# A product over 8 rows widened to 128 rows with zeros, and two transfers of a slotted tensor sent in the other order

## The chip, the cores and the metric

The kernel runs on one core of a Trainium2 chip. The metric is the device time of one execution in microseconds (us), the median of several runs. Engines are named as in the profile: PE (TensorE, matmuls), PEld (its weight loads), DVE (VectorE), ACT (ScalarE), POOL (GpSimd) and SP (SyncE, which here issues nearly all DMAs, and shows as SPq).

## What is computed

The input x is 8 batches of 512 tokens by 128 features, float32. Two layers follow each other:

```
xn = layernorm(x)
x  = x + [xa + concat(linear_attention(h), window_attention(h)) @ Wout] + ternary_ffn(xn)      # layer 0; h = rmsnorm(xa), xa = xn
xn = layernorm(x)
x  = x + causal_attention(LN(xn) ...) @ Wo + bo + sum_e gates[t,e] * (gelu(xn @ W1[e] + b1[e]) @ W2[e] + b2[e])   # layer 1
```

`gates` has, for each token, the softmax of the two largest of eight router logits and zero for the other six experts. The part `gates @ b2`, an (512 x 8) by (8 x 128) product for each batch, is computed apart from the experts' matrices, together with the causal attention's output projection `attn @ Wo`.

## The kernel before

Everything is written engine by engine, with semaphores set by hand. Work runs batch by batch, in a software pipeline. One pass of the loop over the batches (`Fori(1, LAST)`, six passes, b = 1 to 6) does four stages in this order on every engine:

- `linear_stage`: scores of the linear attention of batch b, and, interleaved, the row maxima (`causal_max`) of the causal attention of batch b-1.
- `causal_stage`: scores and weighing of the causal attention of batch b-1, and the window attention's row maxima of batch b.
- `slide_stage`: window attention's scores of batch b (32 units), and between them the end of batch b-1's causal attention (unit 18: `mix_causal`, which adds `gates @ b2` and `attn @ Wo` in one PSUM bank; DVE's `add_mixed` adds it to `y`, and SP's `store` writes y out), and projections of batch b+1.
- `dense_stage`: the dense feed-forward layers of batch b+1 and the projections k2 and q2 for the causal attention of batch b.

Around the loop stand an opening, a first pass without a batch before it, a last pass, and a tail with the causal attention of batch 7 alone. `mix_causal` so runs eight times: six in the loop, once in the last pass, once in the tail. After the tail come 78 expert tiles (`expert_tiles`, `load_tiles`, `add_tile`), which start once the last y is stored.

`mix_causal` (lines 624 to 633) issues, for each of four token tiles t of 128, first the product of `gatesT` and `b2` (line 631, 8 rows) and then that of `attnT` and `wo1` (line 632, 128 rows), both into the same 128 x 128 part of the bank. Every float32 matmul is two MATMUL records with two LDWEIGHTS in the profile, so the unit is 16 records. `weigh` (line 609) follows three units later with the fourth and third pair of heads' probabilities, for which it waits on POOL's `mask_slide` (lines 1097 and 1099) and DVE's `mask_middle` (line 1333).

Heads are laid out in slots of 32 rows by way of DRAM. For q2 and k2, ACT's `split_hi` writes the high part of the projection from PSUM to SBUF (k2 first, then q2), DVE's `split_lo` the rest, and SP then does the following. `split_and_send` waits for the high part, issues two DMAs of it, waits for the low part and issues a third (lines 395 to 402, 256 KB each). `fetch` reads the slots back: k2 in four DMAs (line 406, 192 KB each), q2 in one of 1024 KB (line 408). In the end of SP's `body` the order is: send k2, send q2, fetch k2 (after all three sends of k2 have landed), fetch q2 (after those of q2), wait for that fetch to land, fetch q1 of the next batch. PE waits for both k2 and q2 (`slots_k2`, `slots_q2`) ahead of the first `causal_max`: in `linear_stage` after a lead of 12 linear units, the third layer among them, and in `tail_stage` with nothing but `prefix` ahead.

At the start POOL clears buffers (lines 1205 to 1210) and raises `cleared`; ACT issues 21 loads of later weights (line 1049). DVE waits for `cleared` ahead of line 1599.

Of the kernel before, what the change touches and what calls it, by code (L numbers as in the profile page):

```python
# [15 lines left out]
P = 128  # L16
NB, T = 8, 512
# [5 lines left out]
FC = 4  # L23
E = 8
# [18 lines left out]
SETUP_LOADS, FIRST_LOADS, LATER_LOADS, EXPERT_LOADS = 5, 10, 21, 2  # L43
# [165 lines left out]
def build(nc, dram, out):  # L209
    with ExitStack() as ctx:  # L210
        def sb(name, shape, dt=F32, where=ctx):
            return where.enter_context(nc.sbuf_tensor(name, shape, dt))
# [10 lines left out]
        bv1, bo1 = (sb(n + "_s", [P, P]) for n in ("bv1", "bo1"))  # L223
        wq1, wk1, wv1, wo1 = (sb(n + "_s", [P, P]) for n in ("wq1", "wk1", "wv1", "wo1"))
        wgT = sb("wgT_s", [P, E])
        b1, b2 = sb("b1_s", [P, E * FC]), sb("b2_s", [E, P])
        ident = sb("ident_s", [P, P])
        causal_neg, slide_neg = sb("causal_neg_s", [P, T], BF16), sb("slide_neg_s", [P, WQ], BF16)
        slide_top = sb("slide_top", [P, WIN])
        earlier = sb("earlier_s", [P, E * E])  # L230
# [17 lines left out]
        lg, lgs, ex, exs, gates, rank = (sb(n, [P, NT, E]) for n in ("lg", "lgs", "ex", "exs", "gates", "rank"))  # L248
        above, equal = (hrow[:, n:n + 2, :].rearrange("p a (b e) -> p (a b) e", e=E * E) for n in (0, 2))
        m1, gsum, rsum = (sb(n, [P, NT]) for n in ("m1", "gsum", "rsum"))  # L250
        gatesT = sb("gatesT_s", [E, T])

        picks, place = sb("picks", [P, NT + 1, K2 * E]), sb("place", [P, NT, K2 * E])
        base, base0 = sb("base", [P, K2 * E]), sb("base0", [P, K2 * E])
# [64 lines left out]
        S = {name: ctx.enter_context(nc.semaphore(name)) for name in counts}  # L319


        def due(name, sequence, count):
            (b, ahead), each = sequence, counts[name]
            return b * each + (ahead * each + count)
# [11 lines left out]
        def full_sem(run, unit):  # L336
            return S[f"full{PLACE[run[0]][unit][0]}"]

        def taken_sem(run, unit):
            return S[f"taken{PLACE[run[0]][unit][0]}"]  # L340

        def full_at(run, unit):
            return in_bank(run, unit) + 1

        def taken_at(run, unit):
            return in_bank(run, unit) + 1

        def bank_of(run, unit):
            return bank[PLACE[run[0]][unit][0]]
# [23 lines left out]
        def _(sp):  # L373
# [22 lines left out]
            def send(name, part, slots):  # L396
                view = scratch[name].rearrange("h (s d) t -> s h d t", d=D)
                for s in slots:
                    sp.dma_start(view[s], part.bitcast(F32)).then_inc(S[f"sent_{name}"], 16)
# [10 lines left out]
            def split_and_send(run, sequence, name):  # L410
                halves = parts_of[name]
                sp.wait_ge(S[f"hi_{name}"], due(f"hi_{name}", sequence, 1))
                send(name, halves[0], (0, 2) if name in ("k1", "k2") else (0, 1))
                sp.wait_ge(taken_sem(run, name), taken_at(run, name))
                send(name, halves[1], (1,) if name in ("k1", "k2") else (2,))

            def fetch_sent(sequence, name):
                sp.wait_ge(S[f"sent_{name}"], due(f"sent_{name}", sequence, SENT))
                fetch(name)

            def place_max(run, unit, mrow, to, sem):
                sp.wait_ge(taken_sem(run, unit), taken_at(run, unit))
                for i in range(HG):
                    row = ROWS * i + 3 * D
                    sp.dma_start(to[row:row + 1, :, :].rearrange("p g (n t) -> p (g n) t", t=P).bitcast(F32),  # L425
                                 mrow[G * NT * i:G * NT * (i + 1), :].bitcast(F32)).then_inc(S[sem], 16)

            def store(run, result_of):
                sp.wait_ge(taken_sem(run, "mixed_causal"), taken_at(run, "mixed_causal"))
                sp.sem_inc(S["unread"], 1)  # L430
                sp.dma_start(out_v[result_of], y[:, :, :]).then_inc(S["stored"], 16)

            def load_x(after_norm_of, which):
                sp.wait_ge(S["xa_ready"], due("xa_ready", after_norm_of, 1))
                sp.sem_inc(S["unread"], 1)
                sp.wait_ge(S["xn1"], due("xn1", after_norm_of, 1))
                sp.sem_inc(S["unread"], 1)
                sp.wait_ge(S["hrow1"], due("hrow1", after_norm_of, 1))
                sp.sem_inc(S["unread"], 1)
                sp.dma_start(x_in[:, :, :], x_v[which]).then_inc(S["x_loaded"], 16)  # L440

            def body(run, before, this, after):
                part, b = run
                if before and this:
                    place_max(run, "causal_max", mrow_c, Q2, "placed_c")
                if this:
                    place_max(run, "slide_max", mrow_s, Q1, "placed_s")
                if after:
                    for name in ("q1", "k1", "qm1"):
                        split_and_send(run, (b, 1), name)  # L450
                if this and after:
                    load_x((b, 1), (b + 2) & (NB - 1))
                if before and this:
                    store(run, b - 1)
                if after:
                    if this:
                        sp.wait_ge(taken_sem(run, SLIDE_UNITS[-1]), taken_at(run, SLIDE_UNITS[-1]))
                    fetch_sent((b, 1), "k1")
                    fetch_sent((b, 1), "qm1")
                if this:  # L460
                    split_and_send(run, (b, 0), "k2")
                    split_and_send(run, (b, 0), "q2")
                    if before:
                        sp.wait_ge(S["heads_out1"], due("heads_out1", (b, -1), G))
                        sp.sem_inc(S["unread"], 1)
                    fetch_sent((b, 0), "k2")
                    if after:

                        sp.wait_ge(S["sent_q1"], due("sent_q1", (b, 1), SENT))
                        sp.sem_inc(S["unread"], 1)  # L470
                    fetch_sent((b, 0), "q2")
                if after:

                    if this:
                        sp.wait_ge(S["slots_q2"], due("slots_q2", (b, 0), 16))
                        sp.sem_inc(S["unread"], 1)
                    fetch_sent((b, 1), "q1")
# [23 lines left out]
            set_keys("k1", "keys1_cleared", 2)  # L501
            load_x((0, 0), 1)
            body(("opening", -1), *PARTS["opening"])
            set_keys("k2", "keys2_cleared", 1)
            body(("first", FIRST), *PARTS["first"])
            with sp.Fori(1, LAST) as b:
                body(("steady", b), *PARTS["steady"])
# [405 lines left out]
        def _(act):  # L913
# [120 lines left out]
            def weigh_tile(i):  # L1034
                act.wait_ge(S["tile_out_full"], i + 1)
                if i >= OB:
# [3 lines left out]
            later_loads = [(sh1[:, :], dram["sh1"]), (h1T[:, :, :], dram["h1T"].rearrange("(c p) n -> p c n", p=P)),  # L1040
                           (sh2[:, :], dram["sh2"]), (h2T[:, :, :], dram["h2T"].rearrange("(c p) n -> p c n", p=P)),
                           (s3, dram["s3"].partition_broadcast(P)), (w3T[:, :, :], dram["w3T"].rearrange("(c p) n -> p c n", p=P)),
                           (wout[:, :, :], dram["wout"].rearrange("a p n -> p a n")), (gamma[:, :], dram["gamma"]), (beta[:, :], dram["beta"]),
                           (wq1[:, :], dram["wq1"]), (wk1[:, :], dram["wk1"]), (wv1[:, :], dram["wv1"]), (bq1[:, :], dram["bq1"]), (bk1[:, :], dram["bk1"]),
                           (bv1[:, :], dram["bv1"].partition_broadcast(P)), (wgT[:, :], dram["wgT"]), (b1[:, :], dram["b1"]),
                           (bo1[:, :], dram["bo1"].partition_broadcast(P)), (earlier[:, :], dram["earlier"]), (b2[:, :], dram["b2"]),
                           (wo1[:, :], dram["wo1"])]
            for dst, src in later_loads:
                act.dma_start(dst, src).then_inc(S["later_weights"], 16)  # L1049
            assert len(later_loads) == LATER_LOADS  # L1050
            act.wait_ge(S["setup_done"], 1)
            act.wait_ge(S["first_weights"], 16 * FIRST_LOADS)
            slide_stage(("opening", -1), False, False, True)
# [22 lines left out]
        def _(pool):  # L1076
# [130 lines left out]
            pool.memset(V2[:, :, :, D:D + 1], 1.0)  # L1207
            pool.memset(euler[:, :, :], math.e)
            pool.memset(causal_neg[:, 0:T - P], 0.0)
            pool.memset(half_neg[:, :], -0.5).then_inc(S["cleared"], 1)  # L1210
            pool.wait_ge(S["setup_done"], 1)
            power((0, 0), 1)
# [19 lines left out]
        def _(dve):  # L1232
# [27 lines left out]
            def take(run, unit, to, view=lambda x: x[:, :]):  # L1260
                dve.wait_ge(full_sem(run, unit), full_at(run, unit))
                dve.tensor_copy(to, view(bank_of(run, unit))).then_inc(taken_sem(run, unit), 1)
# [190 lines left out]
                                         in1=hidden_a[c], op0=ALU.mult, op1=ALU.mult).then_inc(taken_sem(run, f"up{c}"), 1)  # L1453

            def take_gates(run):
                take(run, "gatesT", gatesT[:, :], lambda x: x[0:E, :])

            def linear_stage(run, before):
                _, b = run
# [217 lines left out]
```

## Time and profile before

| | us |
|---|---|
| Median of 3 runs | 1498.56 |
| Lowest, highest | 1495.23, 1499.37 |
| Profiled execution | 1501.17 |
| Span of its trace | 1499.3 |
| PE busy | 1330.5 (89%) |
| DVE, ACT, POOL busy | 817.6, 707.5, 603.3 |
| Mean granted TensorE clock | 0.934 |

The span is the time from the first to the last instruction of the profiled execution; 1.9 us lie around it. Start times in the rows below are us from the start of the span. A busy time is that of an engine's instructions; matmuls overlap, so the starts of neighbouring matmuls tell more than the durations.

### The profile page before, as it was taken

To read this page: it belongs to the slowest core of one execution; us is meant where nothing else is said; L and a number is where in the kernel's file an instruction comes from. 1 tells how busy PE (TensorE), PEld (TensorE's weight loads), DVE (VectorE), ACT (ScalarE), POOL (GpSimd) and SP (SyncE) were. 2 spreads that over 40 slices of the span, in tenths; PEclk is the share of its full clock that TensorE was granted. 3 is DMA by queue.
4 is the path that set the end of the run, shared out by engine and by line. 5 is a ranking of instruction groups with operands and counts; after the bars stand their busy time and mean duration, and the time that the engine had idled before them with its cause. 6 is when DMAs were issued, how large, how long until landed. Compare 5 with 4: busy or idle time off the path is not lost.

```text
span 1499.3 us, 28932 instructions
## 1 busy us (share of the span) xinstructions
PE 1330.5 (89%) x9122; PEld 917.4 (61%) x9122; DVE 817.6 (55%) x3372; ACT 707.5 (47%) x1511; POOL 603.3 (40%) x791
## 2 busy tenths in 40 slices
PE   5979999989998999989998999899989965679997
PEld 2545567656664666466656665566566743459997
DVE  3064377537753676367635753486357545436654
ACT  2435247524761466246623662366235610437765
POOL 6123334323441334143414342343243435228787
PEclk9988999999999899999998999899999975789999
DMA  9203310331023202330233022402240025014343
GB/s 263 79 2 97 94 58 9 104 101 54 8 84 95 77 9 79 83 95 10 79 76 102 10 79 50 126 11 72 57 123 13 3 70 179 7 31 66 57 65 47
DMA packets 82246, 102.07 MB, mean 68 GB/s; under 512 B 12472, under 2 KB 43104, under 8 KB 82016
## 3 DMA queue, kind: packets, MB, share of 16 engines
q1 hardware_dynamic: 63616, 86.53, 20.9%
q0 software_dynamic: 14304, 10.61, 4.5%
q10 hardware_dynamic: 4176, 3.01, 0.7%
q8 instruction: 84, 1.38, 0.4%
q14 instruction: 66, 0.54, 0.1%
HBM read 55.44 MB, written 46.37 MB: 68 GB/s over the span
## 4 chain that ended last, share of the span: by engine, by line
PE 61%; issue 14%; DVE 11%; POOL 4%; DMA 3%; ACT 2%; SPq 2%; ACTq 1%; another core or an unknown queue 1%; POOLq 0%; DVEq 0%
PE bank L552 16%; PE bank L545 16%; PE heads L609 11%; PE bank L534 6%; PE bank L530 3%; POOL out L1146 3%; DVE hrow L1284 2%; PE bank L649 2%; DVE hT_s L1284 2%; DVE xnT_s L1284 2%; SPq L425 1%; PE bank L539 1%; DVE mx_c L1284 1%; ACT probs L926 1%; ACTq L1049 1%
## 5 line engine op out<-in xcount | busy, mean ns | idle before, releaser
L926 ACT ACTIVATE probs<-bank 128x512 f32<-128x512 f32 (+2 forms) x896 | 442.5, 574 | 421.8 <-PE bank L552 419.2
L552 PE MATMUL bank<-K,Q 128*128 128x192 f32 (+4 forms) x1024 | 237.0, 323 | 37.8 <-DVE mx_c L1284 12.7
L1084 POOL TENSOR_SCALAR_AFFINE_SELECT probs<-probs 128x384 f32<-128x384 f32 x256 | 127.8, 523 | 325.4 <-ACT probs L926 299.7
L552 PE MATMUL bank<-Q,K 128*128 128x192 f32 (+4 forms) x1024 | 216.9, 328 | 16.1 <-DMA Q<-mrow_c 9.8
L552 PEld LDWEIGHTS bank<-K,Q 128*128 128x128 f32 x1024 | 172.3, 197 | 81.1 <-DVE mx_c L1284 35.1
L609 PE MATMUL heads<-probs,V 128*9 128x192 f32 (+4 forms) x3072 | 205.3, 410 | 15.4 <-DVE probs L1333 5.5
L552 PEld LDWEIGHTS bank<-Q,K 128*128 128x128 f32 x1024 | 155.3, 201 | 46.5 <-issue 24.0
L552 PE MATMUL bank<-QM,K 128*128 128x512 f32 (+3 forms) x512 | 141.9, 366 | 29.1 <-issue 18.9
L609 PEld LDWEIGHTS heads<-probs,V 128*9 128x9 f32 x3072 | 77.6, 93 | 132.7 <-issue 90.4
L1146 POOL DMA_INDIRECT out<-h1T_s x78 | 123.3, 1581 | 52.2 <-ACT h1T_s L1038 27.7
L916 ACT ACTIVATE probs<-bank,sh_s 128x512 f32<-128x512 f32 x64 | 44.0, 688 | 202.6 <-PE bank L545 202.6
L545 PE MATMUL bank<-probs,h2T_s 128*128 128x512 f32 x256 | 127.9, 643 | 4.8 <-ACT probs L916 4.8
L552 PEld LDWEIGHTS bank<-QM,K 128*128 128x128 f32 x512 | 87.2, 201 | 54.7 <-issue 24.1
L1030 ACT ACTIVATE h2T_s<-bank,h1T_s 128x128 f32<-128x128 f32 x312 | 89.2, 368 | 60.9 <-PE bank L859 48.0
L545 PE MATMUL bank<-probs,h1T_s 128*128 128x512 f32 x256 | 115.2, 594 | 1.1 <-DVE probs L1452 1.1
L1105 POOL TENSOR_TENSOR rs<-pw,half_neg 128x4 f32<-128x4 f32 x32 | 32.3, 1020 | 203.8 <-DVE pw L1246 203.8
L1097 POOL TENSOR_SCALAR_AFFINE_SELECT probs<-probs 128x512 f32<-128x512 f32 x64 | 54.9, 858 | 141.5 <-ACT probs L926 141.4
L1130 POOL DMA_INDIRECT sorted_rows<-rows,slot_i x64 | 63.6, 993 | 104.8 <-DVE mx_c L1284 86.1
L1313 DVE COPY ot<-heads 128x512 f32<-128x512 f32 x64 | 44.2, 690 | 101.0 <-PE heads L609 101.0
L545 PEld LDWEIGHTS bank<-probs,h2T_s 128*128 128x128 f32 x256 | 52.2, 211 | 61.6 <-issue 60.9
L859 PE MATMUL bank<-h1T_s,w_in 128*128 128x128 f32 x624 | 83.9, 278 | 0.0
L867 PE MATMUL bank<-w_out,h2T_s 128*128 128x128 f32 x624 | 82.5, 275 | 0.3 <-ACT h2T_s L1030 0.3
(188 smaller groups left out, 2090.3 us busy)
## 6 DMA issues: line engine op xcount, KB each, us to landing
Q<-slots_of_q SPq DMA_DIRECT2D x16, 1024.0 KB, 7.9
slots_of_q<-Q SPq DMA_DIRECT2D x48, 256.0 KB, 3.9
K<-slots_of_k SPq DMA_DIRECT2D x64, 192.0 KB
QM<-slots_of_qm SPq DMA_DIRECT2D x8, 1024.0 KB, 9.2
slots_of_k<-QM SPq DMA_DIRECT2D x24, 256.0 KB, 4.1
slots_of_qm<-Q SPq DMA_DIRECT2D x24, 256.0 KB, 4.3
slots_of_k<-Q SPq DMA_DIRECT2D x24, 256.0 KB, 3.0
h1T_s<-sorted_rows SPq DMA_DIRECT2D x78, 65.0 KB
```

The lines of the kernel that those rows point to most:

```text
L534: pe.matmul(to_bank(run, unit)[:, :], w, x, start=True, stop=True).then_inc(full_sem(run, unit), 1)
L545: mm = pe.matmul(to[:, :], w[:, k, c * P:(c + 1) * P], src[k], start=(k == 0), stop=(k == FC - 1))
L552: mm = pe.matmul(to[:, at:at + right.shape[1]], left, right, start=True, stop=True, skip_group_check=True)
L609: mm = pe.matmul(heads[ROWS * i:ROWS * i + D + 1, P * j:P * j + widths[j]], V[:, j, HG * g + i, :], slot_of(kind, 2 * g + i // 2)[:, at:at ...
L859: mm = pe.matmul(tile_hidden_bank(i)[:, c * P:(c + 1) * P], w_in[:, i % WB, c * P:(c + 1) * P], tile_xT[:, i % 2, :], start=True, stop=True)
L867: mm = pe.matmul(tile_out_bank(i), tile_hidden[i % 2][:, c * P:(c + 1) * P], w_out[:, i % WB, c * P:(c + 1) * P], start=c == 0, stop=c == ...
L926: return act.activation(to, bank, func, scale=scale, bias=bias).then_inc(taken_sem(run, unit), 1)
L1030: last = act.activation(tile_hidden[i % 2][:, c * P:(c + 1) * P], tile_hidden_bank(i)[:, c * P:(c + 1) * P], ACT.Gelu, bias=tile_b1[:, i % ...
L1084: pool.affine_select(out=three, in_=three, compare_op=ALU.is_ge, fill=0.0, base=0, pattern=[[0, 3], [1, P]], channel_multiplier=-1)
L1130: pool.indirect_dma_start(out=sorted_rows, out_offset=bass.IndirectOffsetOnAxis(ap=slot_i[:, n:n + 1], axis=0), in_=rows[:, n // K2, n % K ...
L1146: pool.indirect_dma_start(out=out.rearrange("b t d -> (b t) d"), out_offset=bass.IndirectOffsetOnAxis(ap=tile_rows[:, i % XB, P + 1:P + 2] ...
L1284: last = dve.tensor_tensor_reduce(beside[:, at:at + n], bank_of(run, unit)[:, at:at + n], mask, 1.0, NEG, ALU.add, ALU.max, mx[:, to:to + 1])
```

## The change

`b2` and `gatesT` get 128 rows instead of 8. POOL clears both ahead of `cleared`, so rows 8 to 127 stay zero; the load of `b2` and DVE's copy of the transposed gates write the first 8 rows, as before. The load of `b2` goes to the end of ACT's loads, behind a wait for `cleared`. The text of `mix_causal` is unchanged, and its product over `gatesT[:, ...]` and `b2[:, :]` runs over 128 rows. Apart from that, SP's `body` sends q2 before k2; the fetches keep their order, k2 and then q2.

```diff
-        b1, b2 = sb("b1_s", [P, E * FC]), sb("b2_s", [E, P])
+        b1, b2 = sb("b1_s", [P, E * FC]), sb("b2_s", [P, P])
...
-        gatesT = sb("gatesT_s", [E, T])
+        gatesT = sb("gatesT_s", [P, T])
...
                 if this:
+                    split_and_send(run, (b, 0), "q2")
                     split_and_send(run, (b, 0), "k2")
-                    split_and_send(run, (b, 0), "q2")
...
-                           (bo1[:, :], dram["bo1"].partition_broadcast(P)), (earlier[:, :], dram["earlier"]), (b2[:, :], dram["b2"]),
-                           (wo1[:, :], dram["wo1"])]
+                           (bo1[:, :], dram["bo1"].partition_broadcast(P)), (earlier[:, :], dram["earlier"]), (wo1[:, :], dram["wo1"])]
             for dst, src in later_loads:
                 act.dma_start(dst, src).then_inc(S["later_weights"], 16)
-            assert len(later_loads) == LATER_LOADS
+
+            act.wait_ge(S["cleared"], 1)
+            act.dma_start(b2[0:E, :], dram["b2"]).then_inc(S["later_weights"], 16)
+            assert len(later_loads) + 1 == LATER_LOADS
...
             pool.memset(causal_neg[:, 0:T - P], 0.0)
+            pool.memset(b2[:, :], 0.0)
+            pool.memset(gatesT[:, :], 0.0)
             pool.memset(half_neg[:, :], -0.5).then_inc(S["cleared"], 1)
...
             def take_gates(run):
-                take(run, "gatesT", gatesT[:, :], lambda x: x[0:E, :])
+                take(run, "gatesT", gatesT[0:E, :], lambda x: x[0:E, :])
```

## Rows read from the trace of the kernel before

**Rows 1.** The page: busy time of each engine; the chain that ended last, by engine.
```profile
PE 1330.5 (89%) x9122; PEld 917.4 (61%) x9122; DVE 817.6 (55%) x3372; ACT 707.5 (47%) x1511; POOL 603.3 (40%) x791
PE 61%; issue 14%; DVE 11%; POOL 4%; DMA 3%; ACT 2%; SPq 2%; ACTq 1%; another core or an unknown queue 1%; POOLq 0%; DVEq 0%
```

**Rows 2.** Timeline, start us, us, engine line, operation, count: mix_causal of pass 3.
```profile
589.45 0.48 PE L631 MATMUL bank<-b_s,gatesT_s 8*128 8x128 f32 x2
589.87 0.49 PE L632 MATMUL bank<-wo_s,attnT 128*128 128x128 f32 x2
...
592.60 0.67 PE L552 MATMUL bank<-Q,K 128*128 128x192 f32 x4
```

**Rows 3.** Timeline, same pass: 16 records all over 128 rows, and what follows them.
```profile
621.46 1.95 PE L641 MATMUL bank<-wout_s,attnT 128*128 128x128 f32 x16
623.24 5.32 PE L545 MATMUL bank<-probs,h2T_s 128*128 128x512 f32 x12
```

**Rows 4.** Timeline, same pass: POOL's mask and the weighing that waits for it.
```profile
591.16 0.66 POOL L1099 TENSOR_SCALAR_AFFINE_SELECT probs<-probs 128x512 f32<-128x512 f32 x1
593.20 1.38 PE L609 MATMUL heads<-probs,V 128*9 128x192 f32 x32
```

**Rows 5.** Timeline: the first product of the tail's mix, and what follows the last.
```profile
1326.17 0.48 PE L631 MATMUL bank<-b_s,gatesT_s 8*128 8x128 f32 x2 [0.78 <-DVE attnT L1262]
...
1330.11 0.69 DVE L1446 TENSOR_TENSOR y<-bank,y 128x512 f32<-128x512 f32 x1 [3.99 <-PE bank L632]
1330.89 0.40 SPq L431 DMA_DIRECT2D out<-y  x1
```

**Rows 6.** Windows from a mix to the next dense layer (second last columns: PEclk, DMA share).
```profile
589.40:599.90 10.50, 9.75 (x113) 7.59 (x112) 5.52 (x11) 6.03 (x17) 6.49 (x8) 1.00 0.09 27
892.60:907.00 14.40, 14.40 (x112) 10.93 (x112) 5.32 (x11) 6.63 (x16) 6.14 (x8) 0.64 0.07 19
```

**Rows 7.** Timeline of the tail: ACT's part of q2, SP's sends and fetches, PE's start.
```profile
1226.43 1.84 SPq L399 DMA_DIRECT2D slots_of_k<-Q  x3
1227.42 0.69 ACT L916 ACTIVATE Q<-bank,bq_s 128x512 fp32r<-128x512 f32 x1 [1.02 <-PE bank L534]
1228.32 1.95 SPq L399 DMA_DIRECT2D slots_of_q<-Q  x3
1230.77 2.27 SPq L406 DMA_DIRECT2D K<-slots_of_k  x4
1234.11 0.38 SPq L408 DMA_DIRECT2D Q<-slots_of_q  x1
1242.37 4.07 PE L552 MATMUL bank<-K,Q 128*128 128x512 f32 x12 [5.64 <-issue]
```

**Rows 8.** Timeline and source view: fetches issued back to back in pass 3, the second's landing.
```profile
600.50 1.57 SPq L406 DMA_DIRECT2D K<-slots_of_k  x4
DMA to landing us min/median/max: 8.7/8.7/8.7
```

**Rows 9.** Timeline, between two passes: q2's fetch lands when q1's is issued.
```profile
190.93 0.38 SPq L408 DMA_DIRECT2D Q<-slots_of_q  x1
194.84 0.68 PE L552 MATMUL bank<-K,Q 128*128 128x512 f32 x3
...
648.27 0.38 SPq L408 DMA_DIRECT2D Q<-slots_of_q  x1
653.18 0.68 PE L552 MATMUL bank<-K,Q 128*128 128x512 f32 x3
```

**Rows 10.** Timeline of the start.
```profile
4.47 0.45 POOL L1209 MEMSET causal_neg_s<- 128x384 bf16 x1
...
12.63 0.29 DVE L1599 COPY wqm_s<-bank 128x128 f32<-128x128 f32 x1 [0.95 <-PE bank L886]
```

**Rows 11.** Lines 631 and 632: duration ns min/median/max of the weight loads.
```profile
L631 PEld LDWEIGHTS bank<-b_s,gatesT_s x64: 181/182/277, 282.2 to 1328.8; 8*128 8x128 f32 x64
L632 PEld LDWEIGHTS bank<-wo_s,attnT x64: 186/189/333, 282.6 to 1329.4; 128*128 128x128 f32 x64
```

## Prediction

> **What bounds the kernel now.** I read the page's busy times first, and then the chain that ended last [rows 1]. PE is busy for 1330.5 us of 1499.3, and 61% of the chain is PE's own work; the next largest share is 14% of "issue". No other engine has more than 55%. So time taken out of PE's stream counts, unless something else is late at just that place, and an operation added on SP or DMA counts only where PE has nothing left to do ahead of its result. That gives two places to look at: the eight runs of mix_causal, and each place where PE waits for k2 and q2.
>
> **The mix, six passes of the loop.** The timeline of pass 3 [rows 2] shows the two products of mix_causal alternating. Neighbouring starts lie 0.42 us apart (589.45, 589.87), for two records each; the whole unit goes from 589.45 to the next unit's start at 592.60, which is 3.15 us for 16 records. The unit mix_first has 16 records too, float32, 128 x 128 by 128, alternating between two operands in the same bank, but all over 128 rows. It goes from 621.46 to the next start at 623.24, 1.78 us [rows 3]. With the 8 rows widened to 128, mix_causal is of the same form as mix_first, so I price it at 1.78 us: 3.15 - 1.78 = 1.37 us less. The reading is that each change between 8 and 128 rows costs 0.42 - 0.22 = 0.2 us; one more of them, on entry, would make it 1.57 us, the upper bound.
>
> What is late next is the weighing three units on. It starts at 593.20, and waits for POOL's mask, which ends at 591.16 + 0.66 = 591.82 [rows 4] and is fed by scores from before the mix, so it doesn't move. Some 0.05 us for the semaphore leaves 591.87, so this place gives back at most 593.20 - 591.87 = 1.33 us. Of the 1.37 us I count 1.33, in each of the six passes and in the last one, which has the same 16 records: 7 x 1.33 = **9.3 us**. Behind it PE leads again: ACT and DVE wait there for PE's scores, and the dense layers follow, so I see no place that would swallow it. If one exists, the term falls toward nothing; that is the second rival below.
>
> **The mix in the tail.** Here the mix is on the path by itself: it starts at 1326.17, DVE's addition follows at 1330.11, the store at 1330.89, and the experts' tiles wait for that store [rows 5]. That is 3.94 us. At the duration of mix_first, 1.95 us [rows 3], **2.0 us** less. All eight runs give **11.3 us**. The lower bound of this term is zero, the upper 7 x 1.57 + 2.2 = 13.2 us.
>
> **The swap, in the tail.** SP now waits for the high part of q2 before its first send. ACT ends it at 1227.42 + 0.69 = 1228.11, while k2's first send left at 1226.43 [rows 7]. Queued behind this wait are k2's own sends, whose data has been ready since. q2's three issues take 1.95 us, to 1230.1, then k2's take 1.84, to 1231.9; the last is issued at about 1231.3. k2's last send was issued at about 1227.7 before, and the fetch that waits for it began at 1230.77, 3.1 us later; for q2's last, at 1229.6, it was 4.5 us, with the fetch of k2 already in the queue. I take 3.5, behind six sends and ahead of any fetch: the fetch of k2 begins at 1234.8 instead of 1230.77, 4.0 us later. Its four issues take 2.27 us, and q2's fetch, whose sends have landed by then, follows at 1237.1 instead of 1234.11, 3.0 us later. By the rate of the queue, a pair of fetches issued back to back needs 1.6 us plus 8.7 to land [rows 8], 10.3 us; here the issues are slower by 0.7, so 11.0 from 1234.8, which is 1245.8 against 1242.37, 3.4 us. Between 3.0 and, with a landing of 4.5 us, 5.0 us, I take **3.6 us lost**. PE has waited for nothing but this for 5.64 us [rows 7], so it all counts, and the causal maxima, the gates, the rows sent and the masks of the tail follow PE. The experts' weights are issued behind it too, 3 us later; they are used only after the last store, at 1330.89.
>
> **The swap, in the seven other places.** The same shift arises at every pass's end. Take the end of pass 3: q2's fetch has landed at 648.27, where SP, which waits for it, issues q1's, and PE's first causal_max is at 653.18, behind the third layer [rows 9]. That is 4.9 us of cover. The smallest of the seven is 3.9 us (190.93 to 194.84). The shift of the landing is expected to be the tail's 3.4 us. So the term is **nothing**, with a bound of 7 x 1.1 = 8 us if every landing moved by the full 5.0 us and found only the smallest cover. q1's fetch is moved by the same amount, and its first reader is slide_max, 40 pairs later.
>
> **The start.** Two memsets more on POOL: the 128 x 384 one takes 0.45 us [rows 10], so the two together, 640 columns of twice the width, take an estimated 0.7 to 1.5 us, and `cleared` comes later by that, at 6 to 7. The first to need it is DVE's copy, at 12.63 [rows 10], and ACT waits for it behind 20 loads: hidden, with over 5 us of cover on DVE. ACT issues as many loads as before, and then one wait that is fulfilled: 0.1 us at most, lost. DVE's copy of the gates still writes 8 rows, nothing.
>
> **The sum.** 9.3 + 2.0 - 3.6 - 0.1 = 7.6 us less. The profiled execution's 1501.17 would become 1493.6, of which 1.9 lie around the span. It stands 2.6 us above the median of the runs; from the median, 1498.56 - 7.6 = 1491.0.
>
> **What the clock may add.** The granted clock is not steady at the mix. In pass 3 it was 1.00 (2.4 GHz) from the mix to the next dense layer, and that took 10.5 us; in pass 5 it was 0.64, so at 1.2 GHz for part of it, and that took 14.4 [rows 6]. Denser products and other starts can take away or bring such a stretch, up to 3.9 us each. I can't say which way, and so leave it to the range, some 3 us each way.
>
> **Rivals.** First, the 8 rows aren't what costs the time: then all of the mix stays, and only the swap and the start remain, 1498.56 + 3.7 = 1502.3, which is not told from no change. Against it stands mix_first, which alternates operands in the same manner at 0.11 us a record [rows 3]; for it, only that the operands are other tensors. Weight loads of 8 rows take 182 ns and those of 128 rows 189 [rows 11], so the loads themselves don't differ; the distances between starts do, and I go by these. Chance 0.09. The Trainium skill has a rule that speaks for this rival, in TensorE: Matmul & The Clock Gate, section LDWEIGHTS: a weight load's time goes by its columns and not by its rows, so 8 rows should cost what 128 do. By it nothing is saved and the time would be this rival's; the trace agrees on the loads.
>
> Second, PE's time is saved, and part is lost at a wait that I haven't seen, or to one more slow stretch of the clock: half of 11.3 and the swap, 1498.56 - 5.65 + 3.7 = 1496.6, no change. For it speaks that the mask bounds the gain closely already, against it that PE leads from there on. Chance 0.15.
>
> Third, the other side: the swap costs at every pass's end. The fetch of k2 begins only behind six sends, and the landing of q2 moves by more than the third layer and its lead cover. It decides from a shift of 3.9 us on in one pass, and from 4.9 in the pass shown; 4.4 is the middle. At a shift of 7 us the seven lose 7 x 2.6 = 18.2 us, and the tail 3.4 more: 1491.0 + 21.6 = 1512.6, slower. Against it, 7 us would be a landing of the sends some 3.5 us above any that rows 7 show. Chance 0.06.
>
> Fourth, the swap is free (the fetches land in the tail as before, since the queue is the limit and not the order): 1498.56 - 11.3 + 0.1 = 1487.4. Against it, SP's order lets k2's fetch begin later whatever the rate. Chance 0.1.
>
> **The numbers.** The forecast has the remaining 0.6. The range goes from the fourth rival's 1487.4 less 2.9 for the clock, to the second rival's 1496.6 and up to 1499.5, short of the first rival's 1502.3: 1484.5 to 1499.5. About 0.3%, 4.5 us, is what a measurement of this kernel can tell from no change. Faster by more than that: 0.6 + 0.1, and a little of the second rival, 0.73. Slower: the third rival and a part of the first, 0.08. The same: 0.19.
>
> **What would show it.** In the new trace line 631 should have the form 128*128, starts 0.22 us apart instead of 0.41, and the mix of pass 3 should take 1.8 us to the next unit. The weighing should start within 0.1 us of POOL's mask. SP should issue slots_of_q before slots_of_k, and in the tail PE should start 3 to 5 us further behind q2's projection than now. At the other pass ends, q1's fetch should be issued 2 to 4 us later relative to PE's first causal_max, and still ahead of it. The prediction is wrong if starts on lines 631 and 632 stay 0.4 us apart, or if PE's first causal_max waits for a fetch in the loop.

## The result

The changed kernel takes 1483.12 us (median of 4 runs, 1482.03 to 1483.63), the kernel before 1498.78 us (median of 4, 1495.23 to 1499.37). The ratio is 0.9899, with a 95% interval from 0.9882 to 0.9917: 15.7 us or 1.0% faster. Forecast were 1491.0 us and a range from 1484.5 to 1499.5. The direction was right, and the forecast gain of 7.6 us was half of what came. A second measurement, in a group with other kernels, gave 0.9891 (0.9864 to 0.9918).

The page of the kernel after, its busy times, and the row with the clock that was granted in 40 slices of the span:

```profile
span 1480.7 us, 28934 instructions
PE 1309.8 (88%) x9122; PEld 907.2 (61%) x9122; DVE 817.6 (55%) x3372; ACT 706.2 (48%) x1511; POOL 603.9 (41%) x793
PEclk9988999999999899989998999899989975789999
```

PE's busy time fell by 20.7 us with the same 9122 matmuls, and that of its weight loads by 10.2; DVE's, ACT's and POOL's stayed within 1.3 us [rows 1]. The span is 18.6 us shorter; this pair of profiled executions shows 2.9 us more than the medians. The chain that ended last breaks off in the experts' tiles in this profile, so I compare the timelines instead.

The mix of pass 3 after, from the timeline (start us, us, engine, line, operation, count), which answers to [rows 2] and [rows 4]:

```profile
582.91 0.45 PE L552 MATMUL bank<-Q,K 128*128 128x192 f32 x2
583.19 0.41 PE L631 MATMUL bank<-b_s,gatesT_s 128*128 128x128 f32 x2
583.44 0.39 PE L632 MATMUL bank<-wo_s,attnT 128*128 128x128 f32 x2
583.66 0.39 PE L631 MATMUL bank<-b_s,gatesT_s 128*128 128x128 f32 x2
...
584.92 0.67 PE L552 MATMUL bank<-Q,K 128*128 128x192 f32 x4
585.00 0.65 POOL L1101 TENSOR_SCALAR_AFFINE_SELECT probs<-probs 128x512 f32<-128x512 f32 x1
585.75 1.38 PE L609 MATMUL heads<-probs,V 128*9 128x192 f32 x32 [0.16 <-issue]
```

The products start 0.22 us apart instead of 0.42. The mix takes 584.92 - 583.19 = 1.73 us instead of 3.15. The weighing starts 0.10 us behind POOL's mask, which ends at 585.65: it now waits for that mask, as the forecast said.

To see where the 18.6 us went I measured the distances between fixed points of PE's timeline, in both profiles: the first record of mix_first (a), the third layer of the next pass (b), the mix (c), and the first dense layer h1 (d).

| Stretch, summed | before | after | difference |
|---|---|---|---|
| start to the first mix_first | 164.00 | 163.82 | -0.2 |
| a to b, seven times | 194.11 | 194.46 | +0.4 |
| b to c, seven times | 637.27 | 634.35 | -2.9 |
| c to d, six passes | 68.81 | 54.64 | **-14.2** |
| d to a, six passes | 130.3 | 130.3 | 0.0 |
| c to a in the last pass | 18.91 | 16.56 | -2.4 |
| a of the last pass to the tail's first causal_max | 28.98 | 31.17 | **+2.2** |
| that to the tail's mix | 83.80 | 83.69 | -0.1 |
| the tail's mix to the last store | 4.72 | 2.87 | -1.9 |
| store to the end | 168.41 | 168.82 | +0.4 |

The line that decides is c to d. By pass it was 10.29, 11.85, 10.29, 10.29, 14.19 and 11.90 us before, and 9.10 to 9.12 in every pass after. So each pass gave back 1.19 us at an equal clock, 7.1 us in six, and passes 2, 5 and 6 gave 1.56, 3.90 and 1.61 us more, 7.1 us together. These are the passes in which the clock fell behind the mix. The windows from the mix to the next dense layer (us, busy time and count of PE, PEld, DVE, ACT and POOL, then granted clock, DMA share and GB/s) show it for passes 2 and 6 of the kernel before; pass 5 stands in [rows 6]:

```profile
435.10:447.20 12.10, 11.34 (x113) 8.50 (x112) 5.57 (x11) 6.14 (x17) 6.50 (x8) 0.86 0.08 23
1049.30:1061.40 12.10, 11.34 (x112) 8.47 (x112) 5.53 (x11) 6.12 (x16) 6.51 (x8) 0.86 0.08 23
```

And for passes 2, 5 and 6 of the kernel after:

```profile
432.60:441.70 9.10, 8.17 (x112) 6.92 (x111) 5.39 (x11) 6.07 (x17) 6.50 (x8) 1.00 0.11 31
886.30:895.40 9.10, 8.18 (x113) 6.93 (x112) 5.36 (x11) 6.12 (x17) 6.46 (x8) 1.00 0.10 31
1036.90:1046.00 9.10, 8.17 (x112) 6.92 (x112) 5.38 (x11) 6.08 (x17) 6.49 (x8) 1.00 0.11 31
```

0.86 and 0.64 are means of a clock that stands at either 1.00 (2.4 GHz) or 0.50 (1.2 GHz) within the window.

The 7.1 us belong to one profiled execution, and other executions have other falls. How much slower time there is over all of them can be estimated from the mean granted clock that each run lists. The kernel before has 0.9374 and 0.9381 on average over two groups of 17 runs; four kernels with 128 rows in the same two groups (`rows_only`, and the changed kernel, `rows_again` and `tail_k2_again`, below) have 0.9402 to 0.9410 over 24. With two levels only, that is 186 us at 1.2 GHz before and 176 after, 10 us less. Where PE leads, each of these costs half of itself, so my estimate of the clock's share in the medians is some 5 us.

### The profile page after: what moved, and what is told of

The parts are those of the page before. It is cut to its first block and busy times, and to the rows that moved or that the text cites. A ratio compares the mean times of both kernels' runs of the same rounds, so it can differ in the third digit from the quotient of the medians.

```text
span 1480.7 us, 28934 instructions
## 1 busy us (share of the span) xinstructions
PE 1309.8 (88%) x9122; PEld 907.2 (61%) x9122; DVE 817.6 (55%) x3372; ACT 706.2 (48%) x1511; POOL 603.9 (41%) x793
## 3 DMA queue, kind: packets, MB, share of 16 engines
q8 instruction: 84, 1.38, 0.4%
## 5 line engine op out<-in xcount | busy, mean ns | idle before, releaser
L552 PE MATMUL bank<-Q,K 128*128 128x192 f32 (+4 forms) x1024 | 212.5, 322 | 15.1 <-DMA Q<-mrow_c 9.4
L609 PE MATMUL heads<-probs,V 128*9 128x192 f32 (+4 forms) x3072 | 201.9, 405 | 17.0 <-DVE probs L1337 6.2
L552 PEld LDWEIGHTS bank<-Q,K 128*128 128x128 f32 x1024 | 151.3, 196 | 45.3 <-issue 23.7
```

What stands on the lines that cost most here:

```text
L552: mm = pe.matmul(to[:, at:at + right.shape[1]], left, right, start=True, stop=True, skip_group_check=True)
L609: mm = pe.matmul(heads[ROWS * i:ROWS * i + D + 1, P * j:P * j + widths[j]], V[:, j, HG * g + i, :], slot_of(kind, 2 * g + i // 2)[:, at:at ...
```

## The experiments

The theory after the result (A): the widened rows do it all. They take the gaps, 0.2 us at each change between 8 and 128 rows, out of the mix, and without them PE's clock no longer falls behind the mix. The rival (B): the swap of the sends moves the fetches and PE's start of each pass against the clock, and that takes the slow stretches away. A further rival to A's second half: it isn't the gaps but the length of the mix. Every ratio below is against the kernel before, run in the same group on the same chip.

### Each part alone

`rows_only` is the changed kernel with the sends as before. `swap_only` is the kernel before with this edit alone:

```diff
+                    split_and_send(run, (b, 0), "q2")
                     split_and_send(run, (b, 0), "k2")
-                    split_and_send(run, (b, 0), "q2")
```

> The change without its second part: 128 rows, k2 sent first as before. Theory A (the rows do it all: 1.2 us at each mix of the loop, and the stretches at 1.2 GHz behind the mix in passes 2, 5 and 6, worth 1.5, 3.9 and 1.6 us, go because of it; the swap only costs in the tail): some 2 us faster than the changed kernel, 1481 us, and no granted clock under 1.00 within 10 us behind the mix in any pass. Theory B (the later sends and fetches of the swap move PE's work against the clock, and that takes the slow stretches away): 1.2 x 7 + 1.4 us off the kernel before, 1489 us, slow stretches behind the mix as before.

> The second part alone: q2 sent before k2, 8 rows as before. Theory A: the kernel before plus 2 to 3 us of the tail, 1501 us, slow stretches behind the mix in some passes. Theory B: 1494 us, no slow stretch behind the mix.

Measured: `rows_only` 1479.32 us, ratio 0.9883 (0.9858 to 0.9907); `swap_only` 1497.97 us, ratio 1.0014 (0.9990 to 1.0038). From mix to dense layer `rows_only` shows 9.10 to 9.12 us in all six passes; `swap_only` shows 10.29 or 10.30 in four and 11.85 and 11.90 in passes 2 and 5. So the rows carry the whole gain, the slow stretches included, and B falls. In `swap_only` PE's first causal_max of the tail came 32.45 us behind mix_first instead of 28.98, 3.5 us later, but the times of its runs don't show a loss of that size clear of their spread. The 128-row kernel's six runs spread over 8 us, the 17 of the kernel before in this group over 12, and the 12 of `swap_only` over 16.

### The change of the row count, or the 8 rows

`grouped8` is the kernel before with the products in another order. Its result is wrong, by a relative 0.031 (I take it that the bank loses part of the sums when four of them are open at once, which I didn't look into), so it serves for its times alone; count, shapes and operands of all products are the same.

```diff
                 for t in range(NT):
-                    o = to[:, t * P:(t + 1) * P]
-                    pe.matmul(o, gatesT[:, t * P:(t + 1) * P], b2[:, :], start=True, stop=False)
-                    mm = pe.matmul(o, attnT[:, CAUSAL, t * P:(t + 1) * P], wo1[:, :], start=False, stop=True)
+                    pe.matmul(to[:, t * P:(t + 1) * P], gatesT[:, t * P:(t + 1) * P], b2[:, :], start=True, stop=False, ...)
+                for t in range(NT):
+                    mm = pe.matmul(to[:, t * P:(t + 1) * P], attnT[:, CAUSAL, t * P:(t + 1) * P], wo1[:, :], start=False, stop=True, ...)
```

> The kernel before, the four products of gates and second biases first and then the four of the output projection, same operands and 8 rows, so two changes of the row count in a mix instead of eight. If it is the change from 8 to 128 rows that costs 0.2 us each: the mix takes 1.8 + 0.4 = 2.2 us instead of 3.15, 7 x 0.95 + 1 = 7.7 us less at least, 1491 us, and 1485 if the slow stretches of the clock go too. If a product over 8 rows is slow by itself: mix of 3.1 us, 1499 us.

Measured: 1482.62 us, ratio 0.9890 (0.9866 to 0.9914). Its timeline in pass 3:

```profile
583.95 1.15 PE L630 MATMUL bank<-b_s,gatesT_s 8*128 8x128 f32 x8
585.04 1.16 PE L632 MATMUL bank<-wo_s,attnT 128*128 128x128 f32 x8
585.95 0.67 PE L552 MATMUL bank<-Q,K 128*128 128x192 f32 x4
```

Eight records over 8 rows take 585.04 - 583.95 = 1.09 us, the 0.2 us of one change included, and the eight over 128 rows 0.91. The mix takes 2.00 us. A product over 8 rows is as fast as one over 128; it is the change that costs. Counted from the start of the unit ahead of the mix to that of the unit behind it, it is 3.52 us with eight changes (589.08 to 592.60), 2.37 with two and 2.01 with none, 0.18 to 0.19 us for each change. From mix to dense layer it is 9.14 or 9.15 us in all six passes, no slow stretch.

### How many rows are needed

`rows32` and `rows64` are `rows_only` with 32 and 64 rows in both buffers.

```diff
-        b1, b2 = sb("b1_s", [P, E * FC]), sb("b2_s", [P, P])
+        b1, b2 = sb("b1_s", [P, E * FC]), sb("b2_s", [64, P])
...
-        gatesT = sb("gatesT_s", [P, T])
+        gatesT = sb("gatesT_s", [64, T])
```

> 32 rows instead of 128 for both operands, k2 first. If the time goes by the change between a row count up to 32 and 128: starts 0.41 us apart as with 8 rows, 1497 us, slow stretches in some passes. If any multiple of 32 serves: 1479 us as rows_only.

> 64 rows for both operands, k2 first. If a product is cheap only where it has the row count of its neighbours: starts 0.41 us apart and 1497 us. If more than half of the rows were not needed: 1479 us.

Measured: ratios 0.9991 (0.9965 to 1.0017) and 0.9978 (0.9955 to 1.0001), so no gain that can be told. Two starts of `rows32` and two of `rows64`, pass 3:

```profile
584.97 0.48 PE L631 MATMUL bank<-b_s,gatesT_s 32*128 32x128 f32 x2
585.39 0.49 PE L632 MATMUL bank<-wo_s,attnT 128*128 128x128 f32 x2
```

```profile
588.98 0.49 PE L631 MATMUL bank<-b_s,gatesT_s 64*128 64x128 f32 x2
589.40 0.49 PE L632 MATMUL bank<-wo_s,attnT 128*128 128x128 f32 x2
```

The distance is 0.42 us with either, and a pass's stretch 10.29 to 10.31 us, with one slow stretch (11.91) in `rows32` and none in the profile of `rows64`. Of the four row counts tried, only the 128 of the neighbours takes the gap away; nothing between 64 and 128 was tried.

### Gaps, or length

`dense_long` and `dense_long3` are `rows_only` with each product of gates and second biases issued two and three times, the last overwriting the others, so that the mix is long but without gaps.

```diff
-                    pe.matmul(o, gatesT[:, t * P:(t + 1) * P], b2[:, :], start=True, stop=False)
+                    for _ in range(3):
+                        pe.matmul(o, gatesT[:, t * P:(t + 1) * P], b2[:, :], start=True, stop=False, ...)
```

> 128 rows and k2 first, with each product of gates and second biases issued twice (the second overwrites the first), so 24 records at an even 0.11 us: a mix of 2.7 us, near the 3.15 of before in length, but without gaps. If the slow stretches behind the mix come from the gaps: none, and 7 x 0.9 us more than rows_only, 1488 us. If they come from the mix's length, or from where in time it lies: they are there in some passes, 1492 to 1495 us.

> 128 rows, k2 first, each product of gates and second biases issued three times: 32 records at 0.11 us, a mix of 3.6 us, longer than the 3.15 of the kernel before. If the slow stretches behind the mix come from the gaps between products: none, and the kernel is 8 x 1.78 = 14.2 us slower than rows_only, less what the mask's wait absorbs (0.2 us a pass): 1492 us. If they come from the mix being long: a granted clock under 1.00 behind the mix in two or three passes, 1497 to 1499 us.

Measured: `dense_long` 1485.55 us, 0.9915 (0.9893 to 0.9937), 9.76 or 9.77 us from mix to dense layer in all passes. `dense_long3` 0.9984 to 1.0022 around 1.0003, and 10.65 or 10.66 us in all passes. That is 0.4 us more than the kernel before takes in a pass with the full clock, and still no pass with a fall. Its windows from the mix to h1 in passes 3, 4 and 5:

```profile
583.35:594.01 10.66, 9.90 (x128) 8.64 (x128) 5.41 (x11) 6.08 (x17) 6.49 (x8) 1.00 0.09 26
736.81:747.47 10.66, 9.90 (x128) 8.65 (x128) 5.41 (x11) 6.08 (x17) 6.50 (x8) 1.00 0.10 26
890.29:900.95 10.66, 9.90 (x129) 8.64 (x127) 5.41 (x11) 6.07 (x17) 6.49 (x8) 1.00 0.09 26
```

The number expected for `dense_long3` (1492 us beside 1497.55, 0.4% under the kernel before) was missed by 0.4%. A part of it is in its tail, which took 7.58 us from the mix to the store, against 2.87 in the kernel after: I had put 1.8 more and not 4.7, and the clock's mean in that stretch was 0.59. The rest stays open.

Over all profiles: with eight changes of the row count in a mix (before, `swap_only`, `rows32`, `rows64`) the stretch behind the mix was slow in 3, 2, 1 and 0 of six passes, 6 of 24 in all. With none, or two in `grouped8` (the changed kernel and `rows_only` twice each, `tail_k2_first` and its repetition, `dense_long`, `dense_long3`, `grouped8`) it was slow in 0 of 54.

Not all of these passes can be compared. A fall behind the mix came only in passes in which the clock had fallen once already, some 10 us behind the start of the third layer. That first fall comes with gaps in the mix (12 of 24 passes) and without (17 of 54). Among the 12 there were 6 falls behind the mix, among the 17 none. In all 29 the mix starts 82.1 to 82.7 us behind that first fall, so it isn't the mix's place in time that sets the two groups apart.

### Where the swap costs

`tail_k2_first` is the changed kernel with the old order in the last pass only, where nothing but the tail follows:

```diff
-                    split_and_send(run, (b, 0), "q2")
-                    split_and_send(run, (b, 0), "k2")
+                    for name in ("q2", "k2") if after else ("k2", "q2"):
+                        split_and_send(run, (b, 0), name)
```

> The changed kernel, with k2 sent first again in the last pass alone (the six passes of the loop and the first keep q2 first). If the swap costs only where PE waits for the fetch, in the tail: as rows_only, 1479 to 1480.5 us, and PE's first causal_max of the tail 29.1 us behind the mix of the last pass's heads instead of 31.2. If the swap costs at the loop's end too: 1482 us.

Measured: 0.9890 (0.9859 to 0.9921), PE's first causal_max of the tail 28.99 us behind the last pass's mix_first, instead of 31.17. This group ran on another chip, where the kernel before too took 1479.98 us, so its 1463.32 us can't stand beside the numbers above. I ran the three together once more:

> The changed kernel, for a comparison on one chip with the three others of this group. About 0.990 of the kernel before. If the swap costs nothing, it equals rows_again; if it costs what PE waits longer in the tail, it is 2 to 4 us slower than rows_again.

> 128 rows, k2 first in every pass. If the swap costs in the tail (2.2 us of longer wait): 2 to 4 us faster than after_again. If the first comparison, 1483.1 against 1479.3 us, was between two chips only: equal to it within 1 us.

> k2 first in the last pass alone. If the swap costs in the tail alone: equal to rows_again within 1 us, 2 us faster than after_again. If it costs at the loop's end: equal to after_again less 1 us at most.

Measured: 1480.96, 1481.30 and 1479.57 us; ratios 0.9891 (0.9864 to 0.9918), 0.9894 (0.9867 to 0.9920) and 0.9887 (0.9862 to 0.9912). They aren't told apart. The expectation that `after_again` is 2 to 4 us slower than `rows_again` wasn't met. The longer wait is there in the trace: 31.11 us to the first causal_max in `after_again`, 29.76 and 29.11 in the other two. But both profiles of the changed kernel have a last pass 2.07 us shorter (16.56 and 16.57 us from mix to mix_first, against 18.63 and 18.64 in the k2-first ones), since the clock fell later there. I can't say that the swap causes that. In the pairs of profiles the way to the tail's first causal_max is 1.4 to 3.5 us longer with q2 first; what the swap costs in the total stays open, since the times can't tell it from nothing.

### The mix behind the weighing

`late_mix` is `rows_only` with the mix moved from unit 18 to unit 21, behind the weighing that waits for POOL's mask:

```diff
-    units += ["mixed_causal"] if n == 18 and before else []
+    units += ["mixed_causal"] if n == 21 and before else []
...
-                    if n == 18 and before:
+                    if n == 21 and before:
                         mix_causal(run)
...
-                    if n == 19 and before:
+                    if n == 22 and before:
                         add_mixed(run, previous)
```

> 128 rows, k2 first, and the mix moved behind the weighing, from unit 18 to unit 21 of the window scores (DVE's addition from 19 to 22), so the weighing doesn't wait for POOL's mask behind a mix that got shorter. If that wait bounds the gain of a mix at 1.19 us of 1.37: up to 0.2 us more in six passes, 1 us faster than rows_again. If it only moves the wait (the weighing then comes 1.8 us earlier and waits for the mask instead): the mix's whole 1.8 us doesn't fall under the mask's wait unless the mask ends later than the weighing could start, and the kernel is equal to rows_again or slower by 1 us.

Measured: 1500.34 us, ratio 1.0018 (1.0001 to 1.0035). All of the gain is gone, though the rows are 128, and the expectation (1 us slower than `rows_again` at most) was missed by 18 us. Its timeline in pass 3, and the weighing of pass 1:

```profile
590.06 0.65 POOL L1101 TENSOR_SCALAR_AFFINE_SELECT probs<-probs 128x512 f32<-128x512 f32 x1
590.82 1.38 PE L609 MATMUL heads<-probs,V 128*9 128x192 f32 x32 [1.97 <-issue]
592.40 0.44 PE L631 MATMUL bank<-b_s,gatesT_s 128*128 128x128 f32 x2
594.16 1.09 PE L552 MATMUL bank<-Q,K 128*128 128x192 f32 x8
```

```profile
283.53 2.54 PE L609 MATMUL heads<-probs,V 128*9 128x192 f32 x32 [1.96 <-issue]
286.00 0.69 PE L552 MATMUL bank<-Q,K 128*128 128x192 f32 x2
```

PE now stands idle for 1.97 us ahead of the weighing, because the mask isn't ready (it ends at 590.71, and the weighing starts at 590.82); in its old place the mix, 1.73 us, filled nearly all of that time. In passes 1, 4 and 6 the clock fell behind this wait as well: the same weighing takes 2.54 us instead of 1.38. From the third layer to h1 a pass takes 102.0 us with the full clock and up to 105.1 with a fall; `rows_again` takes 100.3, and 101.7 or 101.8 where the clock has fallen once ahead of the mix. At the full clock these 1.7 us make 10 us in six passes. The mean granted clock of its runs is 0.9359 on average, of `rows_again`'s 0.9403, which by the same estimate as above is 8 us more.

## Why the prediction was wrong

**The mix in the loop: right in kind, 1.19 us for 1.33.** The product over 128 rows is as fast as mix_first's, and the mask is what comes next. The mask itself ends 2.46 us behind the start of the mix instead of 2.37, and the weighing starts 0.10 us behind it instead of 0.05; that is the 0.14. Why the mask ends 0.09 us later isn't shown. Six passes gave 7.1 us; with the last pass, where the weighing came 1.43 us earlier (2.33 instead of 3.76 us behind the mix), 8.5 us for the 9.3 of the forecast. The first rival fell: the changes of the row count do cost the time. The rule that spoke for it, in the Trainium skill, TensorE: Matmul & The Clock Gate, section LDWEIGHTS, is borne out by `grouped8` as far as it goes, since eight records over 8 rows aren't slower than over 128; what the page doesn't speak of there is the change from one row count to the other. TensorEngine Tiling (Array Packing) in the Trainium skill, section Key Properties, does: changing the tiling mode drains the engine. The distances with 8, 32 and 64 rows, 0.42 us each against 0.22, agree with that, if a product over fewer rows counts as another mode. That is my reading, and no run here shows that what costs the time is a drain.

**The clock: this is the step that failed.** The forecast saw that pass 5 was slow behind the mix, gave the clock no term in its sum, and put it into the range as some 3 us each way, "I can't say which way". The trace had a hint: in three of six passes the clock fell in the mix with its gaps, at 437.9, 895.3 and 1052.3 us, and it was the mix that the change made dense. That these falls would go couldn't be read from it. Counted with a sign it is 7.1 us in the profiled executions, as much as the direct saving in the loop. 1491.0 - 7.1 = 1483.9 would have been the forecast, against 1483.1 measured, but that it comes so close is partly luck: the falls behind a mix with gaps cost 7.1, 3.2, 1.6 and 0 us in the four profiles that have such a mix, over all runs the estimate for the clock is some 5 us, and the terms below were off in either direction. That gaps go with falls at this place is shown by 6 of 12 passes against 0 of 17 where a first fall had come, by `dense_long3`, which is longer than the old mix and never falls, and by `late_mix`, where one wait of 1.97 us goes with falls in three passes. What isn't shown is why it strikes one pass and not the next: three of the six passes with gaps that had the first fall alone are in `rows64`, and pass 1 of `late_mix` had only the second.

**The mix in the tail: 1.9 us for 2.0, in part by luck.** In [rows 5] the end of the mix, from 1328.8 us on, runs at a mean clock of 0.51: 0.61 us lie between the starts of the last two products (1328.67 and 1329.28) where 0.42 lie between the others, and 0.83 from the last to DVE's addition where it is 0.42 in the kernel after. The forecast took these 3.94 us as if the clock had been full; some 0.6 of them were the clock's, and 1.3 of the 1.9 are the rows'. In `after_again` and `rows_again`, whose clock was low in the tail's mix, the stretch from it to the store took 4.45 and 4.48 us, against 2.87 here and 4.72 before.

**The swap in the tail: 2.2 us for 3.6.** SP's rows after, which answer to [rows 7]:

```profile
1206.86 0.69 ACT L916 ACTIVATE Q<-bank,bq_s 128x512 fp32r<-128x512 f32 x1 [1.02 <-PE bank L534]
1207.57 1.85 SPq L399 DMA_DIRECT2D slots_of_q<-Q  x3
1209.46 1.92 SPq L399 DMA_DIRECT2D slots_of_k<-Q  x3
1214.74 1.57 SPq L406 DMA_DIRECT2D K<-slots_of_k  x4
1216.36 0.38 SPq L408 DMA_DIRECT2D Q<-slots_of_q  x1
1225.32 2.04 PE L552 MATMUL bank<-K,Q 128*128 128x512 f32 x5 [9.15 <-issue]
```

Counted from mix_first (1194.15 after, 1213.39 before), k2's fetch begins at 20.6 us instead of 17.4, 3.2 us later where I had 4.0. Its four issues take 1.57 us as in [rows 8], not the 2.27 of [rows 7], and q2's fetch isn't held up behind sends any more, so it begins only 1.5 us later (22.2 instead of 20.7), where I had 3.0. The landing takes 9.0 us instead of 8.3. PE's wait grew from 5.64 to 9.15 us, part of it since PE's stretch ahead of it moved. In `swap_only` PE's first causal_max came 3.5 us later than in the kernel before, close to the forecast, so the 2.2 us are one pair's number.

**The swap in the loop: nothing, as forecast, by a hair.** In pass 1, after:

```profile
192.97 0.38 SPq L408 DMA_DIRECT2D Q<-slots_of_q  x1
192.98 0.70 PE L552 MATMUL bank<-K,Q 128*128 128x512 f32 x3
```

q2's fetch has landed at 192.97 and PE's first causal_max starts at 192.98. Of the 3.9 us of cover of [rows 9] none is left in this pass; in the other six 0.7 to 3.8 us are. In the same pass of `after_again` the first causal_max starts 0.78 us behind the unit ahead of it, where it is 0.58 here and 0.55 in `rows_again`: PE waited there for some 0.2 us. The forecast had named such a wait as a sign of being wrong, and it came, too short to count. `swap_only` is not told from the kernel before.

**The start: nothing**, as forecast.

The sum again, for the two profiled executions: 8.5 + 1.9 from the rows, 2.2 lost to the swap, and 7.1 from the clock behind the mix make 15.3 us less; the two spans differ by 18.6, of which 2.9 lie between the third layer and the mix, where falls come in either kernel, in other passes. The medians differ by 15.7. Against these stand the direct terms, 7.6 us without the clock's part in the tail, and the estimate of 5 us for the clock, so some 3 us stay open.

## What to carry to other kernels

Two products that alternate on TensorE should have the same row count: a small one is best padded with zeros to the full 128 rows of its neighbour, where 32 or 64 rows brought nothing; where padding is hard, order the narrow ones together. Small gaps on TensorE can cost twice, once by themselves and, in some passes here, once by the slower clock behind them, so look in the windows at the clock in every repetition of the stage that a change touches, and count a fall that begins there as part of what is removed. Work that stands ahead of a wait is filler for it: moving it behind the wait gave the whole gain back.

## What the runs showed that I hadn't expected

On one of the chips every kernel, the one before included, took some 17 us less: 1479.98 us instead of 1497.6. The profiles put nearly all of it into one stretch, from the tail's first causal_max to its mix: 66.9 us in `rows32` instead of 83.8. In the kernel before, DVE's row maxima there stand still for 1.3 us again and again, between 1259.9 and 1280.9 us:

```profile
1271.13 0.56 DVE L1284 CUSTOM_DVE_ANT_0 hT_s<-bank,causal_neg_s 128x384 bf16<-128x384 f32 x1 [1.32 <-issue]
1273.92 0.29 DVE L1284 CUSTOM_DVE_ANT_0 hT_s<-bank,causal_neg_s 128x128 bf16<-128x128 f32 x1 [1.31 <-issue]
```

In `rows32`, on the faster chip, the same maxima follow each other without such waits:

```profile
1247.36 0.07 DVE L1288 DVE_READ_ACCUMULATOR2_ANT mx_c<- 128x1 f32 x1
1247.36 0.27 DVE L1288 CUSTOM_DVE_ANT_0 hT_s<-bank,causal_neg_s 128x128 bf16<-128x128 f32 x1
```

POOL issues indirect DMAs near these waits in both, but that alone isn't the cause: in the kernel before it issues them from 1247.0 to 1277.2 us, DVE has no such wait in the first 12.8 us of that, and the waits go on for 3.7 us behind it. What differs between the chips I didn't look into. For the comparisons it means that only ratios within a group of runs can be set side by side.
